# Graph attention setup: chunk numbers made on VectorE, searches ahead of the projection's bias, zeros written in block order with a wait per group

## What is computed

```python
def _transformer_conv(x, edge_index, Wq, bq, Wk, bk, Wv, bv, Ws, bs):
    q, k, v = (x @ Wq.T + bq), (x @ Wk.T + bk), (x @ Wv.T + bv)   # each (N, 4 heads, 16)
    logits = (q[dst] * k[src]).sum(-1) / 4
    e = jnp.exp(logits - segment_max(logits, dst)[dst])
    alpha = e / (segment_sum(e, dst)[dst] + 1e-16)
    return segment_sum(v[src] * alpha[..., None], dst) + x @ Ws.T + bs
h = relu(_transformer_conv(LN(x), ...layer 1))
h = relu(_transformer_conv(h, ...layer 2))
x = x + sigmoid(h @ Wo.T + bo)
x = x + ffn(LN(x))      # 8 experts of three 256x256 layers with batch norm, gates by softmax of the mean feature
```

## Time and profile before

| | us |
|---|---|
| median of the timed runs | 3456.58 |
| lowest, highest timed run | 3455.79, 3459.07 |
| profiled execution, span on the core | 3819.9 |
| of it: until the first kv gather (setup) | 197.5 |
| first expert-phase gathers (L1040) | from 2842 on |

### The profile page before, as it was taken

How to read it: one execution, slowest core, us unless ns; L and a number is a source line. 1 busy time by engine, 2 the same in 40 slices (tenths; PEclk the granted TensorE clock), 3 DMA queues, 4 the chain that set the end, 5 groups by cost and what they waited for, 6 DMA issues and landing times. The chain is left out here.

```text
span 3819.9 us, 47527 instructions
## 1 busy us (share of the span) xinstructions
PE 2598.0 (68%) x13194; PEld 2196.2 (57%) x13194; DVE 2277.4 (60%) x3441; ACT 1404.8 (37%) x2768; POOL 1847.1 (48%) x1956
## 2 busy tenths in 40 slices
PE   2446656666666563466666666666658999999999
PEld 1335445555545453344555445445547999899998
DVE  3236666656766672266666666666655655566655
ACT  6212222222222221022222222222226666676665
POOL 6466666666666646666666666666631000000000
PEclk9755666665566665556666666666658999999999
DMA  9344444434444432344444444444420000000000
GB/s 379 100 102 116 113 112 120 116 110 115 118 112 120 113 93 48 84 110 119 121 123 120 122 119 119 124 114 124 120 76 15 21 5 19 23 11 12 20 10 11
DMA packets 364547, 356.12 MB, mean 93 GB/s; under 512 B 58787, under 2 KB 297682, under 8 KB 364454
## 3 DMA queue, kind: packets, MB, share of 16 engines
q1 hardware_dynamic: 191798, 168.12, 14.0%
q0 software_dynamic: 62832, 125.63, 13.4%
q10 hardware_dynamic: 109824, 61.36, 5.4%
HBM read 246.63 MB, written 108.30 MB: 93 GB/s over the span
## 5 line engine op out<-in xcount | busy, mean ns | idle before, releaser
L154 POOL DMA_INDIRECT kv<-kv_table,ix x1664 | 1582.6, 951 | 842.5 <-issue 468.5
L618 DVE TENSOR_TENSOR_SCAN held_q<-mask,held_q,qT 128x512 f32<-128x512 bf16 x208 | 264.1, 1270 | 785.3 <-remote 733.8
L590 PE MATMUL outT<-identity,run_v 128*128 128x128 f32 x832 | 321.7, 387 | 513.6 <-ACT rows L677 434.1
L568 PE MATMUL kT<-identity,kv 128*128 128x128 f32 x832 | 353.6, 427 | 429.7 <-DMA kv<-kv_table,ix 311.1
L590 PEld LDWEIGHTS outT<-identity,run_v 128*128 128x128 f32 x832 | 219.1, 263 | 573.2 <-ACT rows L677 415.0
L662 ACT ACTIVATE drop<-rise 128x512 f32<-128x512 f32 x208 | 130.9, 629 | 935.6 <-DVE rise L638 478.4
L568 PEld LDWEIGHTS kT<-identity,kv 128*128 128x128 f32 x832 | 193.2, 232 | 446.4 <-issue 375.2
L1245 ACT ACTIVATE full_x<-psH_x,offset_x,scale_x 128x448 f32<-128x448 f32 x448 | 333.6, 745 | 260.3 <-PE psH_x L1098 253.0
L1372 DVE TENSOR_TENSOR hid_lo_x<-full_x,hid_hi_x 128x448 fp32r<-128x448 f32 x448 | 276.1, 623 | 253.4 <-ACT hid_hi_x L1245 242.8
L575 PE MATMUL logit<-kq,head_sum 128*128 128x512 f32 x416 | 389.4, 1039 | 22.6 <-issue 15.8
L592 PE MATMUL restT<-pick,top 128*128 128x8 f32 x1664 | 394.5, 310 | 0.0
(11 more groups left out here) (223 smaller groups left out, 5556.6 us busy)
## 6 DMA issues: line engine op xcount, KB each, us to landing
running_sums<-rows ACTq DMA_DIRECT2D x208, 288.0 KB
qz<-q_at_starts SPq DMA_DIRECT2D x208, 256.0 KB
mask<-masks SPq DMA_DIRECT2D x416, 128.0 KB
q_at_starts<-zeros SPq DMA_DIRECT2D x16, 1664.0 KB
kv<-kv_table,ix POOLq DMA_INDIRECT x1664
x_sb<-in_x SPq DMA_DIRECT2D x1, 6272.0 KB
kv_table<-proj SPq DMA_DIRECT2D x14, 448.0 KB
x_x<-in_x POOLq DMA_DIRECT2D x7, 896.0 KB, 5.7
```

The lines of the kernel that those rows point to most:

```text
L154: pool.indirect_dma_start(kv[:, b % UNROLL, j, 2 * HC * s:2 * HC * (s + 1)], None, kv_t, bass.IndirectOffsetOnAxis(ix[:, b, n:n + 1], 0)). ...
L568: pe.transpose(kT[u % 2][:, P * j:P * (j + 1)], kv[:, u, j, 0::2], identity[:, :])
L590: pe.transpose(outT[:, of], run_v[:, u, of], identity[:, :])
L618: dve.tensor_tensor_scan(held_q[:, h, :], mask[:, u, 0, :], qT[:, :], held_q[:, 1 - h, STEP - 1:STEP], ALU.mult, ALU.add).then_inc(q_held, 1)
```

## The change

GpSimd's three operations for the chunk numbers go to VectorE (choose_chunks); GpSimd waits on chunk_set for them. VectorE's statistics loop is written out, with the chunk numbers of groups 0 to 2 ahead of it, those of 3 to 5 between pairs of groups, and those of group 6 after the moments. VectorE searches groups 0 to 3 in a loop before any bias is added, then group 0's bias, search 4, group 1's bias, searches 5 and 6; all other bias additions come after the start rows. TensorE's groups 0 to 2 are written out, and the shift of the starts lies inside group 2, ahead of its sixth transpose. The 16 fills now write q_at_starts in the order of its rows, and eight new operations on VectorE work out, per group, how many rounds of four fills hold all rows to which the group scatters. SP loads that number into a register, waits for it on the four semaphores, adds to fill_there and stores the group's tables; GpSimd's scatters of a group wait on fill_there.

```diff
+        def store_group(sp, projected, per_group, stored, g):
+
+            sp.wait_ge(projected, per_group * g + per_group)
+            sp.dma_start(kv_nodes[:, ts(g, GROUP), :], proj[:, ts(g, GROUP), K0:S0]).then_inc(stored, 16)
+            sp.dma_start(q_nodes[:, ts(g, GROUP), :], proj[:, ts(g, GROUP), Q0:K0]).then_inc(stored, 16)
...
-            FILLS = 16
-            fill = qz_t.rearrange("(p r) c -> p (r c)", p=P).rearrange("p (m k n) -> m p k n", m=FILLS, k=32 // FILLS)
+            FILLS, IN_FLIGHT = 16, 4
+            fill = qz_t.rearrange("(m p k r) c -> m p k (r c)", m=FILLS, p=P, k=32 // FILLS)
+            ROUND = HALF * IN_FLIGHT // FILLS
...
-            filled = [sem(f"filled{n}") for n in range(4)]
+            filled = [sem(f"filled{n}") for n in range(IN_FLIGHT)]
+            fill_wanted_set, fill_passed, fill_there = (sem(n) for n in ("fill_wanted_set", "fill_passed", "fill_there"))
...
-                store_tables(sp, projected, GROUP, stored)
+                sp.wait_ge(fill_wanted_set, 1)
+                for g in range(NG):
+                    filled_by = sp.value_load(fill_wanted[0:1, g:g + 1], min_val=16, max_val=16 * FILLS // IN_FLIGHT)
+                    for fill_part in filled:
+                        sp.wait_ge(fill_part, filled_by)
+                        sp.sem_inc(fill_passed, 1)
+                    sp.wait_ge(fill_passed, IN_FLIGHT * (g + 1))
+                    sp.sem_inc(fill_there, 1)
+                    store_group(sp, projected, GROUP, stored, g)
+                sp.wait_ge(stored, 16 * 2 * NG)
...
                 for g in range(NG):
-                    of = slice(GROUP * g, GROUP * (g + 1))
-                    pool.wait_ge(counted, GROUP * (g + 1))
-                    step(pool.tensor_scalar(chunk_no[:, of], balance[:, of], 0.5, SROWS / 2.0 - 1, ALU.mult, ALU.add))
-                    step(pool.tensor_scalar(chunk_no[:, of], chunk_no[:, of], 0.0, None, ALU.max))
-                    step(pool.tensor_copy(chunk_ix[:, of], chunk_no[:, of]))
+                    pool.wait_ge(chunk_set, g + 1)
...
                 pool.wait_ge(rows_ready, 1)
-                for fill_part in filled:
-                    pool.wait_ge(fill_part, 16 * FILLS // len(filled))
                 for g in range(NG):
+                    pool.wait_ge(fill_there, g + 1)
                     pool.wait_ge(projected, GROUP * (g + 1))
...
-                def group(g):
+                def group(g, between=None):
                     for k in range(GROUP + 1):
+                        if between and k == 5:
+                            between()
...
+                def shift_starts():
+                    pe.wait_ge(started, 1)
+                    pe.matmul(psN[:, 0:NT], shift[:, :], start[:, 0:NT], start=True, stop=False)
+                    pe.matmul(psN[:, 0:NT], wrap[:, :], start[:, 1:NT + 1], start=False, stop=True).then_inc(shifted, 1)
+
                 group(0)
-                with pe.Fori(1, NG // 2 + 1) as g:
-                    group(g)
-                pe.wait_ge(started, 1)
-                pe.matmul(psN[:, 0:NT], shift[:, :], start[:, 0:NT], start=True, stop=False)
-                pe.matmul(psN[:, 0:NT], wrap[:, :], start[:, 1:NT + 1], start=False, stop=True).then_inc(shifted, 1)
-                with pe.Fori(NG // 2 + 1, NG) as g:
+                group(1)
+                group(2, shift_starts)
+                with pe.Fori(3, NG) as g:
                     group(g)
...
+                def choose_chunks(g):
+                    of = slice(GROUP * g, GROUP * (g + 1))
+                    dve.wait_ge(counted, GROUP * (g + 1))
+                    step(dve.tensor_scalar(chunk_no[:, of], balance[:, of], 0.5, SROWS / 2.0 - 1, ALU.mult, ALU.add))
+                    step(dve.tensor_scalar(chunk_no[:, of], chunk_no[:, of], 0.0, None, ALU.max))
+                    step(dve.tensor_copy(chunk_ix[:, of], chunk_no[:, of]))
+                    dve.sem_inc(chunk_set, 1)
+
+                def statistics(g):
+                    for i in range(GROUP * g, GROUP * (g + 1)):
+                        ins = dve.bn_stats(stat[:, i, :], x_sb[:, i, :])
+                    ins.then_inc(stats_done, 1)
+
+                for g in range(3):
+                    choose_chunks(g)
                 dve.wait_ge(x_in, 16)
-                with dve.Fori(0, NG) as g:
-                    for u in range(GROUP):
-                        ins = dve.bn_stats(stat[:, ts(GROUP * g + u, 1), :].rearrange("p i c -> p (i c)"), x_sb[:, GROUP * g + u, :])
-                    ins.then_inc(stats_done, 1)
+                for g in range(3):
+                    statistics(2 * g)
+                    statistics(2 * g + 1)
+                    choose_chunks(3 + g)
+                statistics(NG - 1)
                 dve.wait_ge(stats_done, NG)
                 step_norm = Steps(dve, stats_done, NG)
                 layer_norm_moments(step_norm, mv[:, :, 0], mv[:, :, 1], stat)
                 dve.sem_inc(aggregated, 1)
+                choose_chunks(NG - 1)
                 dve.wait_ge(rooted, 1)
                 step_norm(dve.reciprocal(rstd[:, :], rstd[:, :]))
...
-                with dve.Fori(0, NG // 2) as g:
-                    add_bias(g)
-                    search(2 * g)
-                    search(2 * g + 1)
-                add_bias(NG // 2)
-                search(NG - 1)
+                with dve.Fori(0, 4) as g:
+                    search(g)
+                add_bias(0)
+                search(4)
+                add_bias(1)
+                search(5)
+                search(6)
                 step(dve.memset(start[:, NT:NT + 1], float(E)))
                 step(dve.scalar_tensor_tensor(start[:, 0:NT], chunk_no[:, :], float(SCOLS), found[:, :], ALU.mult, ALU.add))
                 dve.sem_inc(started, 1)
...
+                step(dve.tensor_scalar(in_second[:, :], start[:, 0:NT:GROUP], -1.0, 0.0, ALU.add, ALU.max))
+                step(dve.tensor_scalar(in_second[:, :], in_second[:, :], float(HALF), -float(HALF), ALU.is_ge, ALU.mult))
+                step(dve.tensor_scalar(furthest[:, :], start[:, GROUP:NT + 1:GROUP], -1.0, 0.0, ALU.add, ALU.max))
+                step(dve.tensor_tensor(furthest[:, :], furthest[:, :], in_second[:, :], ALU.add))
+                step(dve.tensor_scalar(rounds[:, :], furthest[:, :], float(ROUND), 1.0, ALU.is_ge, ALU.add))
+                for n in range(2, FILLS // IN_FLIGHT):
+                    step(dve.scalar_tensor_tensor(rounds[:, :], furthest[:, :], float(n * ROUND), rounds[:, :], ALU.is_ge, ALU.add))
+                step(dve.tensor_scalar(fill_wanted[:, :], rounds[:, :], 16.0, None, ALU.mult))
+                dve.sem_inc(fill_wanted_set, 1)
...
-                with dve.Fori(NG // 2 + 1, NG) as g:
+                with dve.Fori(2, NG) as g:
                     add_bias(g)
```

More of the change, by code:

```diff
@@ L160, in gather_early @@
                 gather_block(pool, b)
+        def store_group(sp, projected, per_group, stored, g):
+            sp.wait_ge(projected, per_group * g + per_group)
+            sp.dma_start(kv_nodes[:, ts(g, GROUP), :], proj[:, ts(g, GROUP), K0:S0]).then_inc(stored, 16)
+            sp.dma_start(q_nodes[:, ts(g, GROUP), :], proj[:, ts(g, GROUP), Q0:K0]).then_inc(stored, 16)
         def store_tables(sp, projected, per_group, stored):
             with sp.Fori(0, NG) as g:
-                sp.wait_ge(projected, per_group * g + per_group)
-                sp.dma_start(kv_nodes[:, ts(g, GROUP), :], proj[:, ts(g, GROUP), K0:S0]).then_inc(stored, 16)
-                sp.dma_start(q_nodes[:, ts(g, GROUP), :], proj[:, ts(g, GROUP), Q0:K0]).then_inc(stored, 16)
+                store_group(sp, projected, per_group, stored, g)
             sp.wait_ge(stored, 16 * 2 * NG)
@@ L213, in build @@
             t1 = sb("t1", [P, NT])
+            in_second = sb("in_second", [P, NG])
+            furthest = sb("furthest", [P, NG])
+            rounds = sb("rounds", [P, NG])
+            fill_wanted = sb("fill_wanted", [P, NG], I32)
             shift = sb("shift", [P, P])
@@ L231, in build @@
             zeroed, constants, numbered, made = (sem(n) for n in ("zeroed", "constants", "numbered", "made"))
-            filled = [sem(f"filled{n}") for n in range(4)]
+            filled = [sem(f"filled{n}") for n in range(IN_FLIGHT)]
+            fill_wanted_set, fill_passed, fill_there = (sem(n) for n in ("fill_wanted_set", "fill_passed", "fill_there"))
             chunk_in = [sem(f"chunk_in{g}") for g in range(NG)]
-            pool_step, started, shifted = (sem(n) for n in (
-                "pool_step", "started", "shifted"))
+            chunk_set, started, shifted = (sem(n) for n in (
+                "chunk_set", "started", "shifted"))
             dve_step, stats_done, aggregated, rooted, eps_set = (sem(n) for n in (
@@ L289, in _ @@
                                    pattern=[[CH, P // CH], [0, CH]], channel_multiplier=-1).then_inc(constants, 1)
```

(7 more changed lines are left out.)

## The result

The changed kernel took 3433.69 us (median of four runs, 3429.67 to 3435.03), the kernel before 3457.82 us beside it; the ratio is 0.9934 with a 95% interval from 0.9922 to 0.9945.

A forecast was written before the change was run, and what follows sets the result against it. The setup was taken as the first scatter's start plus 62.9 us plus GpSimd's waits for projections. Gains of 8.8 and 2.5 less 3.9 made 7.4 us: 3456.6 to 3449.2 us, range 3444.5 to 3461.

The forecast's parts named there:

- The reading of the recording: Profiled span 363.3 us above timed runs: most "remote" waits (374.0 us, releaser long done) belong to the recording.
- rival A: Setup: projection stalls under the scatters are real and set the end; 8 us slower, 3464.7 us; chance 0.08.
- part 4: Projections queued behind the start rows: 31 to 35 tiles left, yet each group ready 14 us before its scatters.
- Part 1: Chunk numbers leave GpSimd for VectorE in the setup: last gather at 78.0, gain 8.8 us.
- First search at 73.1: VectorE's first search in the setup starts 4.9 us before the last chunk gather at 78.0.
- Part 2: VectorE's new order of searches and bias additions in the setup: 31.98 us become 29.5, gain 2.5 us.
- Part 3: New hand-over for the zeros before the first scatter, through VectorE and SP: cost 3.9 us.
- the waits for a group's own rows bring nothing: Before the scatters: all zeros landed by 105 us, ahead of the first scatter at 110.0, so no gain.
- rival C: Zeros' DMAs, cut in 256 rows, come slower; at half the rate 45 us slower, 3501 us; chance 0.03.
- Rival D: The change doesn't do what it says; held true for the scatters' waits, since zeros land before; no separate chance.
- rival B: Hand-over or TensorE's late shift eats the searches' gain: 4 us or less remain, 3452.5 to 3456.5 us; chance 0.18.
- The rest follows at the same distance: Everything behind the first scatter moves earlier by the same 7.4 us.

The follow-up runs named there:

- Experiment 3: Changed kernel plus one small GpSimd memset, before the last group's gathers, whose end GpSimd's instruction stream waits for; 3444.31 us, ratio 0.9965 to the kernel before.
- experiment 5: Kernel before with only the new order of VectorE and TensorE; chunk numbers stay on GpSimd, fills as before; 3458.07 us, ratio 1.0002.
- numbers alone: Kernel before with only the chunk numbers moved to VectorE; old order, old fills, one wait for all zeros; 3429.57 us, ratio 0.9925.

## Why the prediction was wrong

**The reading of the recording** was right: no "remote" wait comes back, rival A is false, and part 4's cover is ample (last projection at 138.46 where 150 was forecast: VectorE takes the tiles up at 100.0 and not at 109, and needs 7.7 us a group and not 9).

**Part 1, last gather at 78.0:** 80.30, because the first starts 0.6 us later and four gathers beside the searches take 1.2 to 1.9 us. **First search at 73.1, "since the queue runs ahead" 4.9 us:** this is the step that failed. 64.23 was measured. The 4.9 us were no property of the queue but what was left of it after the wait for group 6's chunk numbers; with that wait gone the stream ran on until 12 gathers, 16 us, lay between it and the gather under way. The part was worth 18 us for the search, not 8.8. Experiment 3 puts one such wait back, and the first scatter comes at 110.98. The forecast is that of a stream that is still held once.

**Part 2:** right. 29.6 us from the first search's start to the last one's end (29.5 forecast); experiment 5 gives 2.9 for 2.5. The shift was not late: TensorE waited 0.6 us for the starts.

**Part 3:** the hand-over was sized well. Start rows at 96.40, first scatter at 100.91, 4.5 us where 4.8 were forecast, SP's share (98.15 to 100.04) 1.9 as worked out. The load, for which no row stood, has one now (source line 278, durations in ns):

```profile
L278 SPq TENSOR_LOAD <-fill_wanted x7: 727/972/1077, 98.2 to 131.3; - x7
```

The first took 1.08 us, where 1.0 was forecast; with the 0.6 us that the prediction gives as the other value its sum would have been too low.

But "the waits for a group's own rows bring nothing" fell with part 1: with start rows at 96.4 the zeros, which keep their rate (rival C is false), would have held the scatters until 106.65. The cost of 3.9 us became a gain of 5.7. Rival D, that the waits are void, is false for the same reason; rival B too.

**"The rest follows at the same distance"** failed twice in opposite directions: the gathers' 8 ns (-12) and the experts' passes (+9). The forecast allowed 2 us for code laid out elsewhere. (Its bounds, added up, give 2.9 to 11.3 us and not 4 to 11; that decides nothing here.) By the first scatter the gain was 17.3 us where 7.4 was forecast; the other 3 us of the recordings' 19.9 are the difference of these two, and the rest up to the timed 24.1 is within the interval.

What the parts are worth by the runs: the chunk numbers carry it. The new order gives 3 us and takes 6 to 9 by its fourth copy of TensorE's code; the zeros' waits give back 5.7 in the setup. Against "numbers alone" the whole change has a setup 7.4 us shorter and is not faster.

## What to carry to other kernels

A lead that one trace shows for an engine's stream is a lead under the waits in it: when a change removes the last wait, count again from the next one, or from how far the queue lets the stream run (12 gathers here). When code of a setup is written out, look far behind it, at the turns of long loops, for waits with no releaser and at the instruction queue's packets; those here cost two to three times what the new order gained. And record the kernel before twice when its span is far from its times: what both recordings share is the kernel.

## What the runs showed of the hardware that was not expected

- GpSimd's stream ran 12 indirect DMAs (16.1 us) ahead of the one under way and no further: from there on it handed over one for each that started, 1.3 us apart instead of 0.54. Held once, it needed 4.0 us for seven gathers and an announcement.
- A loop on TensorE can reload its code at every turn: nine packets of 16 KB, 2.7 us of standing still and then a granted clock of 0.50 (1.2 GHz) for a while, some 4 us a pass of 133.
- The duration of one instruction on GpSimd (952 or 944 ns, 1664 times) depends on what stood between other instructions two milliseconds earlier.
